# Activation tables of ScalarE: one set with logarithm and exponential kept across stages, other sets asked for at the end of the stage before

## The chip, the cores and the metric

The kernel runs on one core of a Trainium2 chip. The time is device microseconds of one execution, from its start to its end on the device. Each kernel is timed in several runs, and the median is compared; one further execution is recorded by the hardware profiler, and all rows below come from it. The engines of the core are TensorE (PE, matrix products; PEld are its weight loads), VectorE (DVE), ScalarE (ACT, activation functions), GpSimd (POOL) and SyncE (SP, which issues most transfers).

## What is computed

One network of six residual layers over an input of 2 x 128 x 32 x 32, all in float32. Cut to the functions that matter here:

```python
x = L0_conv(x)       # offsets: gelu, tanh; bias: log1p, relu MLP; softmax; then an MLP with gelu
x = L1_conv(x)       # group norm (rsqrt), attention with softmax
t = tokens(x)        # 2 x 1024 tokens of 128
t = t + L2_attn(ln(t))   # 8 heads, softmax with relative positions
t = t + L2_ffn(ln(t))    # trajectory of an ODE (RK4 steps), f(y) = tanh MLP of width 512
t = t + L3_attn(ln(t))   # gated linear attention: log_sigmoid gates, exp of sums
                         #   o = o * rsqrt(mean(o*o) + eps) * g_norm_w * (g * sigmoid(g))
t = t + L3_ffn(ln(t))    # 32 experts, top 2 by sigmoid
ln(v) = (v - mean) / sqrt(var + eps)
```

## The kernel before

Everything stays on chip between the layers. The residual X lies as 128 channels x 2048 columns (2 images x 1024 pixels, NB = 2), and most work goes in NCH = 4 chunks of 512 columns (CH), or in tiles of 128 tokens. PSUM is used as eight banks of 512 columns. The program is written by hand, engine by engine: each layer is one or more stages (class Stage), each with one block in which every engine has its own list of instructions and its own semaphores. Between two blocks all engines meet at a barrier, so a stage begins when the slowest engine of the one before is done. Inside a stage, `wait_ge` and `then_inc` on named semaphores set the order; an engine works through its list in order, and Chain (`link`) waits for an instruction's own result before the next.

The stages in order: l0_bias (prepare and scores), l0_attend, l0_mlp, l1_attention, layer_norm "l2a_norm", l2_attention, l2_guess, l2_sweeps, layer_norm "l3a_norm", l3_gates, l3_chunks, l3_gated_output, layer_norm "l3f_norm", l3_experts.

Places that the change touches:

- l0_prepare, L377: Ln of the distances. l0_attend, L840 to L854: for 16 tiles ScalarE makes Exp and, one tile later, copies the turned probabilities to PT; at the end four copies to ATT feed the projection. l0_mlp, L910 to L916: 16 Gelu.
- l1_attention: the group norm's statistics go VectorE, TensorE, VectorE, TensorE; then VectorE adds eps and takes the reciprocal (L990, L991), ScalarE takes the root (L1045), VectorE makes gain and shift (L994 to L996). Later 16 Exp (L1059).
- layer_norm, three times: TensorE centres four chunks (L1174), ScalarE squares them (L1193), TensorE averages the squares (L1178), ScalarE takes four Ln (L1197) and four Exp with scale -0.5 (L1201), VectorE multiplies (L1185).
- l2_guess: a small norm of two start columns (Sqrt at L1726, reciprocal at L1697), then eight rounds with Tanh (L1730, L1733). TensorE runs products that nobody reads (keep_clock, L1744) while it waits. l2_sweeps: Tanh in a loop (L1938); at its end VectorE writes a flag (L2014) that all engines read to decide on a further sweep; one sweep runs.
- l3_gates: Exp and Ln for the gates (L2119, L2120), later Exp of sums (L2125). l3_chunks: ScalarE only copies outputs (L2229).
- l3_gated_output: TensorE makes four gate products (L2303), ScalarE squares four chunks (L2316) in two buffers, so that number 2 waits for the mean of number 0 (L2306); then four Silu (L2319), four Ln (L2323), four Exp (L2326). VectorE goes chunk by chunk: weighted product (L2332), multiply by the root (L2336); then adds to X (L2339). TensorE projects each chunk (L2309).
- l3_experts: Sigmoid at L2470, then Relu and Copy.

Of the kernel before, what the change touches and what calls it, by code (L numbers as in the profile page):

```python
# [15 lines left out]
ALU = mybir.AluOpType  # L16
# [4 lines left out]
NB = 2  # L21
# [47 lines left out]
class Chain:  # L69
# [5 lines left out]
    def __call__(self, ins):  # L75

        ins.then_inc(self.sem, 1)
        self.n += 1
        self.eng.wait_ge(self.sem, self.n)

# [156 lines left out]
def l0_prepare(st, block, X, PS, W, first, rest, KM, VT, Q, A, WORK, NF, x_in, x_dram):  # L238
# [107 lines left out]
    def _(act):  # L346
# [27 lines left out]
        act.activation(mag[:], flat, ACT.Abs).then_inc(sem("mag"), 1)  # L374
        act.activation(sgn[:], flat, ACT.Sign).then_inc(sem("mag"), 1)
        act.wait_ge(sem("mag"), 2)
        act.activation(mag[:], mag[:], ACT.Ln, bias=1.0).then_inc(sem("logs"), 1)  # L377
# [369 lines left out]
def l0_attend(nc, X, PS, W, SALL, VT, loads):  # L747

    with ExitStack() as ctx:
# [90 lines left out]
        @block.scalar  # L840
        def _(act):
            for s in range(TILES + 1):
                if s < TILES:
                    act.wait_ge(sem("shifted"), s + 1)
                    e = E[:, s % 3].rearrange("p g k -> p (g k)")
                    act.activation(e, e, ACT.Exp).then_inc(sem("exp"), 1)
                if s >= 1:
                    act.wait_ge(sem("back"), s)
                    if s >= 3:
                        act.wait_ge(sem("valued"), s - 2)  # L850
                    act.activation(PT[:, (s - 1) % 2], PS[:, 2 + (s - 1) % 2], ACT.Copy).then_inc(sem("pt"), 1)
            for n in range(NCH):
                act.wait_ge(sem("valued"), 16 if n >= 2 else 8)
                act.activation(ATT[:, n * CH:(n + 1) * CH], PS[:, 4 + n], ACT.Copy).then_inc(sem("att"), 1)  # L854

def l0_mlp(nc, X, PS, W, loads):

    with ExitStack() as ctx:
# [49 lines left out]
        @block.scalar  # L909
        def _(act):  # L910
            for g in range(4 * NCH):
                n, k = divmod(g, 4)
                act.wait_ge(sem("up"), g + 1)
                if n >= 2:
                    act.wait_ge(sem("down"), n - 1)
                act.activation(H[:, n % 2, k], PS[:, g % 6], ACT.Gelu, bias=W["mlp_b1"][:, k:k + 1]  # L916
                               ).then_inc(sem("gelu"), 1)

# [18 lines left out]
def l1_attention(nc, X, PS, W, loads):  # L938

    with ExitStack() as ctx:  # L940
# [32 lines left out]
        def _(dve):  # L973
# [15 lines left out]
            dve.wait_ge(sem("group_var"), 1)  # L989
            link(dve.tensor_scalar(rstd[:], PS[:, 1, 0:NB], 1e-6, None, ALU.add))  # L990
            link(dve.reciprocal(rstd[:], rstd[:]))  # L991
            dve.sem_inc(sem("inverse"), 1)
            dve.wait_ge(sem("root"), 1)
# [49 lines left out]
        def _(act):  # L1043
            act.wait_ge(sem("inverse"), 1)
            act.activation(rstd[:], rstd[:], ACT.Sqrt).then_inc(sem("root"), 1)  # L1045
            for n in range(NCH):
# [107 lines left out]

def layer_norm(nc, name, X, XN, PS, centre, mean, eps, loads=None):

    with ExitStack() as ctx:
# [29 lines left out]
        def _(act):  # L1188
# [9 lines left out]
            for n in range(NCH):  # L1198
                c = slice(n * CH, (n + 1) * CH)
                act.wait_ge(sem("log"), n + 1)  # L1200
                act.activation(R[:, c], R[:, c], ACT.Exp, scale=-0.5).then_inc(sem("inverse"), 1)  # L1201

# [459 lines left out]
def l2_guess(nc, X, O, PS, W, NORM, Y0, Y):  # L1663
    with ExitStack() as ctx:
# [21 lines left out]
        def _(dve):  # L1686
# [9 lines left out]
            dve.wait_ge(sem("root"), 1)  # L1696
            link(dve.reciprocal(R[:], R[:]))  # L1697
            link(dve.tensor_tensor(Y0[:], C[:], R[:], ALU.mult))
# [25 lines left out]
        def _(act):  # L1724
            act.wait_ge(sem("var"), 1)
            act.activation(R[:], PS[:, 4, 0:NB], ACT.Sqrt, bias=NORM["eps"]).then_inc(sem("root"), 1)  # L1726
            for g in range(GUESSES):
# [96 lines left out]
def l2_sweeps(nc, X, X2, PS, W, Y0, Y, loads):  # L1824
# [5 lines left out]
    with ExitStack() as ctx:  # L1830
# [96 lines left out]
        def _(act):  # L1927
            end = act.alloc_register("act_end")
            act.reg_mov(end, STEPS_N)
            with act.Fori(0, end) as sweep:  # L1930
# [12 lines left out]
                reg_wait(act, sem("flag"), sweep + 1, sem("act_passed"))  # L1943
                act.reg_load(end, flag[0:1, 0:1])

        @block.vector
# [228 lines left out]
def l3_chunks(nc, PS, W, KE, KD, V, QM, decay, OT):  # L2175

    with ExitStack() as ctx:
# [45 lines left out]
        @block.scalar  # L2223
        def _(act):
            for t in range(ITILES):
                for b in range(NB):
# [58 lines left out]
def l3_gated_output(nc, X, PS, W, XN, OT, loads):  # L2285

    with ExitStack() as ctx:
# [24 lines left out]
        def _(act):  # L2312
            for n in range(NCH):
                if n >= 2:
                    act.wait_ge(sem("ms"), n - 1)
                act.activation(SQ[:, n % 2], OT[:, col(n)], ACT.Square).then_inc(sem("square"), 1)  # L2316
            for n in range(NCH):
                act.wait_ge(sem("g"), n + 1)
                act.activation(G[:, col(n)], PS[:, n], ACT.Silu).then_inc(sem("silu"), 1)  # L2319

            for n in range(NCH):
                act.wait_ge(sem("ms"), n + 1)
                act.activation(R[:, col(n)], PS[:, 4 + n], ACT.Ln, bias=W["eps"]).then_inc(sem("log"), 1)  # L2323
            for n in range(NCH):
                act.wait_ge(sem("log"), n + 1)
# [3 lines left out]
        def _(dve):  # L2329
            for n in range(NCH):  # L2330
                dve.wait_ge(sem("silu"), n + 1)
                dve.scalar_tensor_tensor(G[:, col(n)], G[:, col(n)], W["g_norm"], OT[:, col(n)], ALU.mult,  # L2332
                                         ALU.mult).then_inc(sem("weighted"), 1)
                dve.wait_ge(sem("root"), n + 1)
                dve.wait_ge(sem("weighted"), n + 1)
# [197 lines left out]
def build(nc, x_dram, packs, offsets, out_dram):  # L2533
    with ExitStack() as ctx:
# [87 lines left out]
        W = pack("l3f", l2f)  # L2622
        layer_norm(nc, "l3f_norm", X, XN, PS, W["centre"], W["mean"], W["eps"])
        l3_experts(nc, X, XN, PS, W, out_dram, stored)
# [20 lines left out]
```

## Time and profile before

| | |
|---|---|
| median of 3 runs | 1673.09 us (1671.84 to 1678.54) |
| the profiled execution | 1676.29 us, its span 1674.4 us |
| PE busy | 1500.5 us, 90% of the span |
| DVE busy | 886.2 us, 53% |
| ACT busy | 872.5 us, 52% |
| POOL busy | 320.8 us, 19% |

The span runs from the first to the last instruction that the profiler recorded; the execution's own time has 1.9 us around it. In the rows below, a time in brackets is how long the engine sat idle before the instruction, with what released it. Without brackets the engine went straight on. Rows of the same line are merged where they follow each other (x4 is four instructions, the second number then the time from the first start to the last end).

### The profile page before, as it was taken

The numbers are of one execution on the slowest core, as the hardware profiler recorded it, in microseconds if no ns is written. First come the engines' busy times: TensorE is split into PE (matmuls) and PEld (weight loads), VectorE is DVE, ScalarE is ACT, GpSimd is POOL, SyncE is SP. The second block draws the span as 40 slices with busy tenths as digits, with TensorE's granted clock in tenths as the row PEclk, the third lists the DMA queues.
The fourth block names the chain that finished last, engine by engine and source line by source line (L and its number), as shares of the span: only waits on it lengthen the run. The fifth ranks groups of instructions, "written<-read, shape, count | busy, mean of one in ns | idle before, by whom it ended". The sixth has DMA issues, their size and how long they took to land. (4 is left out here: it accounts for less than half of the span.)

```text
span 1674.4 us, 29793 instructions
## 1 busy us (share of the span) xinstructions
PE 1500.5 (90%) x12334; PEld 739.5 (44%) x12334; DVE 886.2 (53%) x1364; ACT 872.5 (52%) x1292; POOL 320.8 (19%) x139
## 2 busy tenths in 40 slices
PE   6889999999778997999999999899999999939678
PEld 4322222222243774666666666554444444316333
DVE  2578888888772554677777777110002000258243
ACT  3567777777543435677777776232222222250451
POOL 0746666666220001000000000000000000020000
PEclk9589999999998999799999999899999999979899
DMA  1000000000001003444344431000000000000000
GB/s 65 1 2 2 2 2 2 2 2 2 2 22 77 0 1 118 147 150 162 134 173 177 165 151 39 1 1 0 1 0 0 0 0 0 31 0 4 1 1 25
DMA packets 21089, 69.66 MB, mean 42 GB/s; under 512 B 736, under 2 KB 17248, under 8 KB 18656
## 3 DMA queue, kind: packets, MB, share of 16 engines
q1 hardware_dynamic: 20672, 66.76, 10.7%
q8 instruction: 96, 1.57, 0.4%
q10 hardware_dynamic: 288, 1.05, 0.2%
q14 instruction: 33, 0.27, 0.1%
HBM read 33.21 MB, written 34.60 MB: 40 GB/s over the span
## 5 line engine op out<-in xcount | busy, mean ns | idle before, releaser
L553 POOL TENSOR_TENSOR l_work<-l_a_scores,l_work 128x2048 f32<-128x2048 f32 x64 | 232.9, 3640 | 126.5 <-PE banks L673 126.5
L1909 PE MATMUL banks<-s_h,pack_l2f_l3f 128*128 128x512 f32 x512 | 221.0, 592 | 0.0
L1938 ACT ACTIVATE s_h<-banks,pack_l2f_l3f 128x512 f32<-128x512 f32 x128 | 88.0, 688 | 239.2 <-PE banks L1909 175.7
L1510 ACT ACTIVATE r_e<-banks,r_max 128x512 f32<-128x512 f32 x256 | 162.1, 685 | 51.2 <-DVE r_max L1551 51.1
L613 DVE TENSOR_TENSOR l_work<-banks,sc_negc 128x1024 f32<-128x1024 f32 x128 | 156.2, 1221 | 49.6 <-PE banks L720 33.2
L573 ACT ACTIVATE l_work<-banks,pack_l 128x1024 f32<-128x1024 f32 x128 | 142.7, 1115 | 74.7 <-PE banks L673 73.7
L673 PE MATMUL banks<-l_work,pack_l 32*32 32x512 f32 x4096 | 159.6, 606 | 23.5 <-ACT l_work L573 19.8
L1545 DVE TENSOR_REDUCE r_raw<-banks 128x1 f32<-128x640 f32 (+1 forms) x128 | 109.8, 858 | 90.6 <-PE banks L1435 88.9
L1455 PE MATMUL banks<-pack_l2a,r_e 128*128 128x128 f32 x1024 | 147.5, 285 | 10.4 <-ACT r_e L1510 10.2
L1909 PEld LDWEIGHTS banks<-s_h,pack_l2f_l3f 128*128 128x128 f32 x512 | 97.3, 190 | 122.5 <-issue 122.5
L1435 PE MATMUL banks<-r_k,r_q 32*128 32x128 f32 (+3 forms) x832 | 148.8, 466 | 1.1 <-DVE r_v L1379 1.1
L605 DVE TENSOR_TENSOR l_work<-banks,l_a_scores 128x2048 f32<-128x2048 f32 x64 | 146.0, 2281 | 0.7 <-PE banks L666 0.7
L567 ACT ACTIVATE l_work<-l_work 128x1024 f32<-128x1024 f32 x128 | 134.3, 1052 | 9.6 <-POOL l_work L553 9.6
L1455 PEld LDWEIGHTS banks<-pack_l2a,r_e 128*128 128x128 f32 x1024 | 112.0, 142 | 54.7 <-ACT r_e L1510 46.1
L1964 DVE TENSOR_SCALAR s_k<-banks,pack_l2f_l3f 128x512 f32<-128x512 f32 x12 | 9.0, 750 | 221.8 <-PE banks L1914 221.8
L1435 PEld LDWEIGHTS banks<-r_k,r_q 32*128 32x128 f32 x832 | 87.4, 188 | 71.7 <-issue 55.0
L673 PEld LDWEIGHTS banks<-l_work,pack_l 32*32 32x32 f32 x4096 | 42.1, 103 | 138.2 <-issue 103.3
L2136 POOL MEMSET ga_keep<- 128x1024 f32 x1 | 1.0, 951 | 474.0 <-SPq L2067 474.0
L1559 DVE COPY r_pt<-banks 128x512 f32<-128x512 f32 x128 | 87.9, 687 | 4.1 <-PE banks L1455 3.5
L1518 ACT ACTIVATE r_pt<-banks 128x512 f32<-128x512 f32 x128 | 76.5, 597 | 25.1 <-PE banks L1455 25.1
L1420 PE MATMUL banks<-pack_l2a,r_q 32*128 32x257 f32 x224 | 80.1, 437 | 0.0
L1551 DVE CUSTOM_DVE_ANT_0 banks<-banks,r_band,r_raw 128x384 f32<-128x384 f32 (+1 forms) x128 | 75.9, 593 | 6.3 <-DVE r_raw L1545 0.2
(399 smaller groups left out, 2079.1 us busy)
## 6 DMA issues: line engine op xcount, KB each, us to landing
distances<-r_rd SPq DMA_DIRECT2D x16, 2048.0 KB, 6.5
r_band<-distances SPq DMA_DIRECT2D x16, 1536.0 KB, 7.0
pack_l2f_l3f<-pack_dram_l2f SPq DMA_DIRECT2D x1, 2244.5 KB, 10.4
pack_l2f_l3f<-pack_dram_l3f SPq DMA_DIRECT2D x1, 1248.5 KB, 7.0
residual<-x ACTq DMA_DIRECT2D x2, 512.0 KB, 6.1
out<-residual SPq DMA_DIRECT2D x4, 256.0 KB, 2.0
pack_l<-pack_dram_l SPq DMA_DIRECT2D x1, 945.0 KB, 7.5
pack_l2a<-pack_dram_l2a SPq DMA_DIRECT2D x1, 715.0 KB, 5.5
```

Source lines behind the costliest of these rows:

```text
L553: pool.tensor_tensor(image(H1R[:, (c + 1) % 3]), bc(a, 2, 16), bc(b, 3, HW), ALU.add).then_inc(sem("added"), 1)
L567: act.activation(h, h, ACT.Relu).then_inc(sem("relu"), 1)
L573: act.activation(H2R[:, (2 * c + part) % 3], PS[:, RELU:RELU + 2], ACT.Relu, bias=W["cpb_b2"]).then_inc(sem("h2_relu"), 1)
L605: dve.tensor_tensor(image(H1M[:, c % 2]), bc(b, 3, HW), bc(a, 2, 16), ALU.max).then_inc(sem("h1_max"), 1)
L613: dve.tensor_tensor(image(H2M[:, (2 * c + part) % 3]), image(PS[:, MAX + j:MAX + j + 2]), bc(NEGC[:, j:j + 2, n, i, rows(half)], 3, HW), A ...
L673: ins = pe.matmul(PS[32 * u:32 * u + 32, bank], w2(j), h[32 * j:32 * j + 32, u], start=True, stop=True, tile_position=(32 * j, 32 * u))
L1435: ins = pe.matmul(PS[:, 2 * (t % 2) + a, col:col + n * P], Qm[at, a, h % 2, b * PIX + t * P:b * PIX + (t + 1) * P], K[at, a, b, slot:slot ...
L1455: ins = pe.transpose(PS[:, 4 + h, j * P:(j + 1) * P], E[:, t % 2, c:c + P], W["ident"])
L1510: act.activation(E[:, t % 2, a * CH:(a + 1) * CH], PS[:, 2 * (t % 2) + a], ACT.Exp, bias=mx[:, t % 2:t % 2 + 1], scale=-1.0).then_inc(sem( ...
L1545: dve.tensor_reduce(raw[:, one], v[:, lo:hi], AX.X, ALU.min).then_inc(sem("far"), 1)
L1909: ins = pe.matmul(bank, W["w2"][:, col:col + P], H1[:, c, m], start=(m == 0), stop=(m == HB - 1))
L1938: act.activation(H[:, c, k], PS[:, g % 8], ACT.Tanh, bias=bias).then_inc(sem("tanh"), 1)
```

## The change

- That set is asked for ahead of the Ln in l0_prepare, at the end of l0_mlp, at the end of l2_sweeps and in l3_gated_output between Silu and Ln.
- Gelu's set is asked for in l0_attend after the last Exp (in the last turn of the loop, ahead of the last PT copy), Tanh's in l2_guess after the norm, Silu's at the start of l3_chunks, Sigmoid's at the end of l3f_norm.
- The two roots (group norm, l2_guess) become Ln and Exp with scale -0.5 on ScalarE, each waiting for the one before; VectorE's two reciprocals go.
- In l3_gated_output the squares move from ScalarE to VectorE, Ln and Exp alternate chunk by chunk on ScalarE, and VectorE makes all four weighted products ahead of the four multiplies.

```diff
+LOG_EXP, GELU, TANH, SILU, SIGMOID = ("natural_log_exp_and_others", "gelu_and_others", "exp_and_others",
+                                      "silu_and_others", "sigmoid_and_others")
...
         act.activation(sgn[:], flat, ACT.Sign).then_inc(sem("mag"), 1)
+        act.preload_act_table_set(LOG_EXP)
         act.wait_ge(sem("mag"), 2)
...
                     act.activation(e, e, ACT.Exp).then_inc(sem("exp"), 1)
+                else:
+                    act.preload_act_table_set(GELU)
                 if s >= 1:
                     act.wait_ge(sem("back"), s)
...
                 act.activation(H[:, n % 2, k], PS[:, g % 6], ACT.Gelu, bias=W["mlp_b1"][:, k:k + 1]
                                ).then_inc(sem("gelu"), 1)
+            act.preload_act_table_set(LOG_EXP)
...
-            link(dve.tensor_scalar(rstd[:], PS[:, 1, 0:NB], 1e-6, None, ALU.add))
-            link(dve.reciprocal(rstd[:], rstd[:]))
-            dve.sem_inc(sem("inverse"), 1)
+            dve.tensor_scalar(rstd[:], PS[:, 1, 0:NB], 1e-6, None, ALU.add).then_inc(sem("spread"), 1)
             dve.wait_ge(sem("root"), 1)
...
-            act.wait_ge(sem("inverse"), 1)
-            act.activation(rstd[:], rstd[:], ACT.Sqrt).then_inc(sem("root"), 1)
+            act.wait_ge(sem("spread"), 1)
+            act.activation(rstd[:], rstd[:], ACT.Ln).then_inc(sem("log"), 1)
+            act.wait_ge(sem("log"), 1)
+            act.activation(rstd[:], rstd[:], ACT.Exp, scale=-0.5).then_inc(sem("root"), 1)
...
-def layer_norm(nc, name, X, XN, PS, centre, mean, eps, loads=None):
+def layer_norm(nc, name, X, XN, PS, centre, mean, eps, loads=None, table=None):
...
                 act.activation(R[:, c], R[:, c], ACT.Exp, scale=-0.5).then_inc(sem("inverse"), 1)
+            if table:
+                act.preload_act_table_set(table)
...
             dve.wait_ge(sem("root"), 1)
-            link(dve.reciprocal(R[:], R[:]))
...
-            act.activation(R[:], PS[:, 4, 0:NB], ACT.Sqrt, bias=NORM["eps"]).then_inc(sem("root"), 1)
+            act.activation(R[:], PS[:, 4, 0:NB], ACT.Ln, bias=NORM["eps"]).then_inc(sem("log"), 1)
+            act.wait_ge(sem("log"), 1)
+            act.activation(R[:], R[:], ACT.Exp, scale=-0.5).then_inc(sem("root"), 1)
+            act.preload_act_table_set(TANH)
...
                 act.reg_load(end, flag[0:1, 0:1])
+            act.preload_act_table_set(LOG_EXP)
...
         def _(act):
+            act.preload_act_table_set(SILU)
             for t in range(ITILES):
...
             for n in range(NCH):
-                if n >= 2:
-                    act.wait_ge(sem("ms"), n - 1)
-                act.activation(SQ[:, n % 2], OT[:, col(n)], ACT.Square).then_inc(sem("square"), 1)
-            for n in range(NCH):
                 act.wait_ge(sem("g"), n + 1)
                 act.activation(G[:, col(n)], PS[:, n], ACT.Silu).then_inc(sem("silu"), 1)
-
+            act.preload_act_table_set(LOG_EXP)
             for n in range(NCH):
                 act.wait_ge(sem("ms"), n + 1)
                 act.activation(R[:, col(n)], PS[:, 4 + n], ACT.Ln, bias=W["eps"]).then_inc(sem("log"), 1)
-            for n in range(NCH):
                 act.wait_ge(sem("log"), n + 1)
                 act.activation(R[:, col(n)], R[:, col(n)], ACT.Exp, scale=-0.5).then_inc(sem("root"), 1)
 
         @block.vector
         def _(dve):
+            for n in range(NCH):
+                if n >= 2:
+                    dve.wait_ge(sem("ms"), n - 1)
+                dve.tensor_tensor(SQ[:, n % 2], OT[:, col(n)], OT[:, col(n)], ALU.mult).then_inc(sem("square"), 1)
             for n in range(NCH):
                 dve.wait_ge(sem("silu"), n + 1)
                 dve.scalar_tensor_tensor(G[:, col(n)], G[:, col(n)], W["g_norm"], OT[:, col(n)], ALU.mult,
                                          ALU.mult).then_inc(sem("weighted"), 1)
+            for n in range(NCH):
                 dve.wait_ge(sem("root"), n + 1)
...
-        layer_norm(nc, "l3f_norm", X, XN, PS, W["centre"], W["mean"], W["eps"])
+        layer_norm(nc, "l3f_norm", X, XN, PS, W["centre"], W["mean"], W["eps"], table=SIGMOID)
```

## Rows read from the trace of the kernel before

**Rows 1.** The page's first part: busy time, share of span, count of each engine.

```profile
PE 1500.5 (90%) x12334; PEld 739.5 (44%) x12334; DVE 886.2 (53%) x1364; ACT 872.5 (52%) x1292; POOL 320.8 (19%) x139
```

**Rows 2.** Groups of ScalarE by line: count, busy us, mean ns, idle before.

```profile
L1197 ACT ACT_TABLE_LOAD x3 | 3.8, 1283 | 0.1
...
L1197 ACT ACTIVATE l2a_norm_r<-banks,pack_l2a 128x512 f32<-128x512 f32 x4 | 2.4, 688 | 0.0
...
L1201 ACT ACTIVATE l2a_norm_r<-l2a_norm_r 128x512 f32<-128x512 f32 x4 | 2.2, 618 | 0.0
```

**Rows 3.** Order of time in l2a_norm: start us, us, engine, line, operation.

```profile
632.09 2.89 PE L1178 MATMUL banks<-l2a_norm_sq,pack_l2a 128*128 128x512 f32 x6
...
633.82 1.28 ACT L1197 ACT_TABLE_LOAD   x1
...
635.12 2.42 ACT L1197 ACTIVATE l2a_norm_r<-banks,pack_l2a 128x512 f32<-128x512 f32 x4
...
638.85 2.19 ACT L1201 ACTIVATE l2a_norm_r<-l2a_norm_r 128x512 f32<-128x512 f32 x4
639.51 2.48 DVE L1185 TENSOR_TENSOR normed<-banks,l2a_norm_r 128x512 f32<-128x512 f32 x4 [12.10 <-ACT l2a_norm_r L1201]
```

**Rows 4.** Order of time at the end of l0_attend.

```profile
492.53 0.60 ACT L851 ACTIVATE at_pt<-banks 128x512 f32<-128x512 f32 x1 [0.70 <-PE banks L780]
...
493.18 0.30 PEld L787 LDWEIGHTS banks<-at_pt,l_vt 128*128 128x128 f32 x2 [0.65 <-ACT at_pt L851]
```

**Rows 5.** Order of time at the start of l1_attention.

```profile
528.42 1.28 ACT L1045 ACT_TABLE_LOAD   x1 [7.21 <-PEq L859]
...
534.18 0.20 ACT L1045 ACTIVATE gn_rstd<-gn_rstd 128x2 f32<-128x2 f32 x1 [4.47 <-DVEq L992]
```

**Rows 6.** Order of time in l2_guess, behind the norm.

```profile
1055.36 1.28 ACT L1730 ACT_TABLE_LOAD   x1
...
1058.57 1.33 PE L1775 MATMUL banks<-g_y,pack_l2f_l3f 128*128 128x64 f32 x8
```

**Rows 7.** Order of time at the end of l2_sweeps and the start of l3a_norm.

```profile
1454.39 1.49 PE L1875 MATMUL banks<-pack_l2f_l3f 128*128 128x512 f32 x2
1454.60 0.14 DVE L2014 TENSOR_SCALAR s_flag<-banks 1x1 int32<-1x1 f32 x1
...
1456.15 0.50 PEld L1174 LDWEIGHTS banks<-residual,pack_mlp_l3a 128*128 128x128 f32 x2 [1.46 <-issue]
```

**Rows 8.** Order of time in l3_gates, at the gate's logarithm.

```profile
1486.90 1.28 ACT L2120 ACT_TABLE_LOAD   x1
```

**Rows 9.** Order of time in l3_gated_output.

```profile
1564.88 3.73 PE L2306 MATMUL banks<-go_sq,pack_mlp_l3a 128*128 128x512 f32 x8
...
1567.44 1.28 ACT L2319 ACT_TABLE_LOAD   x1
...
1569.37 0.75 DVE L2332 SCALAR_TENSOR_TENSOR go_g<-go_g,pack_mlp_l3a,gl_o 128x512 f32<-128x512 f32 x1 [14.54 <-ACT go_g L2319]
...
1575.85 2.19 ACT L2326 ACTIVATE go_r<-go_r 128x512 f32<-128x512 f32 x4
...
1580.04 0.75 DVE L2332 SCALAR_TENSOR_TENSOR go_g<-go_g,pack_mlp_l3a,gl_o 128x512 f32<-128x512 f32 x1
...
1580.89 0.69 DVE L2336 TENSOR_TENSOR gl_o<-go_g,go_r 128x512 f32<-128x512 f32 x1
1581.50 2.48 DVE L2339 TENSOR_TENSOR residual<-banks,residual 128x512 f32<-128x512 f32 x4
```

**Rows 10.** Slices: stretch, its us, busy us of each engine, granted clock (PEclk), DMA share.

```profile
638.00:640.00 2.00, 0.00 (x0) 0.00 (x0) 0.48 (x1) 1.99 (x4) 0.00 (x0) 0.81 0.00 0
...
644.00:646.00 2.00, 2.00 (x4) 0.83 (x3) 0.00 (x0) 1.27 (x2) 0.73 (x2) 0.50 0.00 0
646.00:648.00 2.00, 1.84 (x5) 0.53 (x3) 1.53 (x3) 0.98 (x2) 0.00 (x0) 0.98 0.00 0
...
1570.00:1572.00 2.00, 0.00 (x0) 0.00 (x0) 0.12 (x1) 1.98 (x3) 0.00 (x0) 0.77 0.00 0
```

## The prediction

> **What bounds the kernel now.** The program is a row of stages with a barrier between them, so the question for each table load is local: did its stage wait for it? The page's first part says that TensorE is busy 90% of the span and ScalarE 52% [rows 1]; taken alone this would say that ScalarE work is worth nothing. That is an average. I went on in three steps. First the groups of ScalarE: loads stand at 17 lines, 21 loads in all (three each at L1197 and L1201, one each at fifteen others), every one 1283 ns, 26.9 us together [rows 2]. Then the order of time around each, to see what the instruction behind the load waited for. Last the granted clock around the gaps that TensorE has there. The reader should see two kinds of load. One starts as soon as the stage opens or the last work is done, and is over before its data comes. The other stands between two instructions that are both ready, with TensorE and VectorE idle behind it.
>
> **Loads that are covered now.** At L1045 the load runs from 528.42 to 529.70, and the square root behind it starts at 534.18, when VectorE has its variance [rows 5]. L1730 has 1055.36 to 1056.64, while TensorE's first product for Tanh starts only at 1058.57, behind its own clock-keeping products [rows 6]. L359, L846, L916, L1059, L1726, L2125 and L2470 look the same: nine loads of this kind. Taking these away, or asking earlier, gains nothing. The loads of L351 and L377 stay in their places. Ten are left.
>
> **Loads on the path.** A normalisation (three of them, here the first) [rows 3]: Square ends at 633.81 and the load follows at 633.82, Ln runs from 635.12 to 637.54, another load, Exp from 638.85, and VectorE multiplies as the Exps come. Between the end of one ACTIVATE and the start of the next lie 1.31 us. Without a load they overlap: four Ln take 2.42 us and not 4 x 0.688 [rows 2, 3], a pitch of 0.58, so an overlap of 0.11. A load on the path is therefore worth 1.31 + 0.1 = 1.4 us, and two are worth 2.8. Would another wait take over? Ln number 3 needs the last variance product, which ends at 634.98 (632.09 + 2.89); after the change it would start at 633.7 + 3 x 0.58 = 635.4. No. Each normalisation: -2.8.
>
> The Trainium skill, page "ScalarE: Activation LUTs", section "What ACT_TABLE_LOAD costs", gives 1283 ns for the load and a drain of 1380 ns beside it, 2.66 us for every switch. The 1283 ns are the trace's too; the drain isn't, since the ACTIVATE behind stands 1.31 us after the one ahead [rows 3]. By the page's figure the switches on the path would be worth near 1.4 us more each, for ten of them 14 us; the measurement decides.
>
> Gates stage: L2120's load (1486.90) stands between two chained activations, Abs/Exp ahead and Ln behind, and VectorE waits. A chained pair without a load has a gap of 0.03, so it gives back 1.28; the V copies behind Ln waited for nothing, and the load of L2125 is covered by VectorE's scan. All later steps hang on the Ln: -1.3 [rows 8].
>
> **The gated output** is where most is. Before: squares on ScalarE, the last waiting for TensorE, load at 1567.44, Silu, load, Ln, load, Exp to 1578.04 (1575.85 + 2.19), last multiply on VectorE 1580.89 to 1581.58, stage's last add ends 1583.98 [rows 9]. After:
> - Squares go to VectorE: 0.69 for such a product [rows 9] against 0.63, and VectorE sat idle for 14.5 us there [rows 9]. The last one still waits for TensorE and ends near 1567.5. Behind that wait stand the four weighted products.
> - Silu no longer waits for squares, only for its own product. The last of these ends as the next product of TensorE begins, 1564.88 [rows 9], plus 0.2: Silu over by 1565.7. The Silu table is asked for in the chunk stage, whose ScalarE has an idle start.
> - The table request: 1565.7 to 1567.0. Only Ln number 0 waits for it; its mean is two passes of 0.43 after 1564.88, 1565.9 with the way to ScalarE.
> - Ln and Exp alternate, each Exp waiting for its Ln: 0.69 + 0.03 + 0.62 - 0.10 = 1.24 per chunk. Exp number 3 ends at 1567.0 + 4 x 1.24 + 0.1 = 1572.05.
> - VectorE: weighted products 1567.5 + 4 x 0.66 + 0.1 = 1570.2 (0.75 each [rows 9], 0.09 overlap); multiplies from there at 0.60, the last waits for Exp number 3: 1572.1 to 1572.8.
> - From the last multiply to the end the stage took 2.40 (four adds, 2.48 from first to last [rows 9]); kept, this gives 1575.2 against 1583.98. -8.7. TensorE needs 4 x 0.86 from 1571.0 at the high clock, 1574.4, just in time. At the low one 1577.8 and the gain is -5.3: the upper bound.
>
> **What the early requests cost.** The load is asked for at the end of a stage, where something may be last already.
> - l0_attend (Gelu): between the second last and the last copy of PT. Before, the last copy waits 0.70 for TensorE and starts at 492.53, and the product behind waits for that copy [rows 4]. The load runs 491.83 to 493.11: copy, last product, projection and adds come 0.6 later. At L916 the load was covered, so nothing is given back: +0.6.
> - l0_mlp: ScalarE sits idle 7.2 us until the next stage opens at 528.42 [rows 5]: 0.
> - Group norm: Ln (0.20) + 0.03 + Exp (0.20) take the place of reciprocal (0.17), a step over and the root (0.20): between -0.1 and +0.3, I take 0 since the two chains are both 0.5 long.
> - l2_guess: +0.03 on VectorE, hidden with the Tanh load behind TensorE until 1058.57 [rows 6]; without that cover 0.03 and 0.
> - End of the sweeps: nothing in the trace shows when ScalarE leaves its loop. The flag is written at 1454.74; the barrier falls 0.27 after TensorE's last product (1454.39 + 1.49 = 1455.88) [rows 7]. ScalarE comes between those two times; with the load it arrives at 1456.1 to 1457.1, that is +0.2 to +1.3. I take the middle, +0.7.
> - l3f_norm (Sigmoid): ScalarE's Exps end 0.95 before VectorE's last multiply (641.04 and 641.99 in the row of the first norm [rows 3]); a load of 1.28 there makes ScalarE last by +0.3. L2470 was covered: nothing back. If the barrier doesn't wait for a load, this term and the one before are 0.
>
> Sum: 3 x (-2.8) - 1.3 - 8.7 + 0.6 + 0.7 + 0.3 = **-16.8 us**. The profiled execution took 1676.29 (span 1674.4), 3.2 above the median of 1673.09; it goes to 1659.5, and the median to **1656.3**.
>
> **The clock.** TensorE's gap of 7.3 us at a norm lets its granted clock fall: it is 0.81 in the mean from 638 to 640, 0.50 (the 1.2 GHz level) in the slices from 640 to 646, and 0.98 behind, with TensorE back at work from 642.3 [rows 10]. So some 3.7 us of work run at half speed, costing 1.8. The change cuts these gaps to 4.5, and that of the gated stage from 8.7 to 2.3. The fall came about 4 us after TensorE stopped at 634.98, at the gated stage some 2.5 us after its last mean (0.77 from 1570 to 1572) [rows 10]; so I count neither gain nor loss in the sum, and put it in a rival.
>
> **Rivals.**
> A. The clock stays at 2.4 GHz through all four gaps: 4 x 1.8 = 7 us more, 1649.3. For it: the gaps are shortened by 38 to 74%. Against: gaps of 4.5 us are still longer than the time the fall took. Chance 0.10.
> B. TensorE becomes the bound of the gated output at the low clock (-5.3 in place of -8.7) and the requests cost their upper bounds (+0.6 more): -12.8, 1660.3. For it: the clock fell 2.5 us after the last product there. Chance 0.13.
> C. Slower: the loads go on being placed by function, and the explicit requests come on top. Before, Ln is given a table without Exp although one with both exists: every Ln and Exp pair of the norms has two loads [rows 2, 3]. Then the alternation in the gated stage takes 0.69 + 1.3 + 0.62 + 1.3 = 3.93 per chunk: from 1568.3 to 1582.7, +4.7 against 1578.04; group norm +1.3, requests +1.6: +7.6, 1680.7. It decides at the second load in front of an Exp. Against: Tanh, Exp, Relu and Copy that a loaded set serves have no load of their own, so a set is kept while it serves. Chance 0.03.
> The Trainium skill's page "ScalarE activation tables: per-element evaluation and per-set limits", section "Table sets in the compiler and the runtime", says that loads are placed for the greedy longest run. By that rule Ln and Exp of a norm would share one load already and the change would gain one and not two per norm. The trace has two [rows 2].
> D. The sweeps stop when the last change is small enough; one sweep now, 336 us. Roots made as exponentials shift the start value a little; if the test failed, a second sweep would give some 1993. It acts on guess and sweep alike, so chance 0.01.
>
> **How the numbers follow.** Forecast 0.73. Its own spread: the runs of before span 6.7 us, and the parts uncertain by a microsecond or two, so about 1652 to 1661. The range reaches to A's and B's sides: **1648 to 1664**. Half a per cent (8.4 us) is what a measurement here can tell from no change. Faster by more (under 1664.7): forecast, A and most of B, 0.92. Within: 0.06. Slower: half of C, and D, 0.02.
>
> **What would show it.** Ten loads and not 21, none at L1197 or L1201's places; norms from Square to first Exp 2.8 shorter; last multiply of the gated stage some 9 us after the last square mean and not 14; a Gelu load ahead of the last PT copy; l3_experts opening behind a ScalarE load. The forecast fails if Ln and Exp are still loaded apart, if TensorE runs low through the gated projection, or if the barrier gaps grow where loads were added.

## The result, and the profile after

| | before | after |
|---|---|---|
| median | 1674.68 us (11 runs, 1671.84 to 1678.54) | 1667.14 us (11 runs, 1663.41 to 1671.83) |
| profiled execution | 1676.29 us, span 1674.4 | 1664.98 us, span 1663.1 |
| PE busy | 1500.5 us | 1504.4 us |
| ACT busy | 872.5 us | 856.3 us |

The ratio is 0.9955, with a 95% interval of 0.9939 to 0.997: faster by 7.5 us where 16.8 were forecast. (Ratios leave disturbed runs out, so they need not equal the quotient of two medians.) The two profiled executions differ by 11.3 us.

The loads did what they should. ScalarE's groups of after by line (count, busy us, mean ns, idle before) have ten loads; these are the requests that stand at the end of a stage, in l0_attend, l2_sweeps and the norm, and the one inside the gated stage:

```profile
L853 ACT ACT_TABLE_LOAD x1 | 1.3, 1283 | 0.0
...
L1957 ACT ACT_TABLE_LOAD x1 | 1.3, 1283 | 3.2 <-DVE s_flag L2027 3.2
...
L2330 ACT ACT_TABLE_LOAD x1 | 1.3, 1283 | 0.0
L1211 ACT ACT_TABLE_LOAD x1 | 1.3, 1283 | 0.0
```

The first norm of after, in order of time (start, us), against [rows 3]: Ln starts while the last Square ends, Exp while the last Ln ends.

```profile
632.36 0.60 ACT L1201 ACTIVATE l2a_norm_sq<-banks 128x512 f32<-128x512 f32 x1 [1.12 <-PE banks L1186]
632.85 2.41 ACT L1205 ACTIVATE l2a_norm_r<-banks,pack_l2a 128x512 f32<-128x512 f32 x4
635.13 2.21 ACT L1209 ACTIVATE l2a_norm_r<-l2a_norm_r 128x512 f32<-128x512 f32 x4
635.82 2.48 DVE L1193 TENSOR_TENSOR normed<-banks,l2a_norm_r 128x512 f32<-128x512 f32 x4 [9.24 <-ACT l2a_norm_r L1209]
```

The gated stage of after, against [rows 9]: the load of the common set at 1565.64, Ln and Exp in turn from 1566.93, VectorE's multiplies from 1570.00, its last add over at 1575.17:

```profile
1561.32 3.67 PE L2317 MATMUL banks<-normed,pack_mlp_l3a 128*128 128x512 f32 x8 [0.63 <-PEq L2190]
...
1565.64 1.28 ACT L2330 ACT_TABLE_LOAD   x1
...
1566.93 0.69 ACT L2333 ACTIVATE go_r<-banks,pack_mlp_l3a 128x512 f32<-128x512 f32 x1
1567.35 2.73 DVE L2345 SCALAR_TENSOR_TENSOR go_g<-go_g,pack_mlp_l3a,gl_o 128x512 f32<-128x512 f32 x4
1567.65 0.63 ACT L2335 ACTIVATE go_r<-go_r 128x512 f32<-128x512 f32 x1
...
1570.00 2.72 DVE L2350 TENSOR_TENSOR gl_o<-go_g,go_r 128x512 f32<-128x512 f32 x4
...
1570.74 3.70 PE L2323 MATMUL banks<-gl_o,pack_mlp_l3a 128*128 128x512 f32 x8 [2.13 <-DVE gl_o L2350]
...
1572.64 2.53 DVE L2353 TENSOR_TENSOR residual<-banks,residual 128x512 f32<-128x512 f32 x4
```

Where, then, did the rest go? With a barrier between stages the two traces can be laid side by side, stage by stage. The table gives each stage's length, from the moment when the last engine reached the end of one block to the same moment of the next, and behind it how long TensorE had the low clock in it (granted 0.50, 1.2 GHz). All in us:

| stage | before | low | after | low | difference |
|---|---|---|---|---|---|
| l0_bias | 443.62 | 51.2 | 442.68 | 58.0 | -0.94 |
| l0_attend | 53.85 | 6.8 | 54.38 | 6.8 | +0.54 |
| l0_mlp | 29.62 | 0 | 29.62 | 0 | 0 |
| l1_attention | 99.28 | 10.2 | 98.83 | 6.8 | -0.45 |
| l2a_norm | 14.41 | 1.9 | 11.55 | 0 | -2.86 |
| l2_attention | 410.24 | 25.5 | 408.31 | 20.5 | -1.9 |
| l2_guess | 63.42 | 6.8 | 71.07 | 23.9 | **+7.65** |
| l2_sweeps | 340.96 | 0.7 | 340.96 | 0.4 | 0 |
| l3a_norm | 14.96 | 4.7 | 14.40 | 7.6 | -0.56 |
| l3_gates | 26.27 | 9.2 | 25.43 | 11.8 | -0.85 |
| l3_chunks | 62.16 | 12.7 | 63.19 | 14.4 | +1.03 |
| l3_gated_output | 23.92 | 13.7 | 13.75 | 0 | -10.2 |
| l3f_norm | 14.63 | 2.7 | 11.49 | 0 | -3.1 |
| l3_experts | 75.25 | 4.2 | 75.59 | 3.4 | +0.34 |

The differences sum to the 11.3 us. Without l2_guess they are 19.0. In l2_guess the instructions are nearly the same; the clock isn't. The whole stage in one slice (length, busy us of PE, PEld, DVE, ACT, POOL, then the granted clock), first before, then after:

```profile
1051.32:1114.74 63.42, 58.01 (x417) 38.71 (x418) 13.09 (x35) 16.69 (x53) 0.00 (x0) 0.95 0.00 1
```

```profile
1045.70:1116.77 71.07, 65.67 (x417) 43.05 (x418) 12.92 (x34) 16.14 (x53) 0.00 (x0) 0.83 0.00 1
```

The same stage of after in order of time. Its clock-keeping products (L1756) run from 1049.01 to 1052.68, and the sixteen products of L1797 take 3.68 us in each of the first two rounds:

```profile
1049.01 3.67 PE L1756 MATMUL banks<-pack_l2f_l3f 128*64 128x256 f32 x8
...
1052.61 1.97 PE L1787 MATMUL banks<-g_y,pack_l2f_l3f 128*128 128x64 f32 x8
...
1055.56 3.68 PE L1797 MATMUL banks<-pack_l2f_l3f,g_h 128*64 128x256 f32 x16
...
1067.22 3.68 PE L1797 MATMUL banks<-pack_l2f_l3f,g_h 128*64 128x256 f32 x16
```

In before the clock-keeping products (L1744) took the same 3.67 us, but the sixteen products of the first round (L1785) took 1.95:

```profile
1054.97 3.67 PE L1744 MATMUL banks<-pack_l2f_l3f 128*64 128x256 f32 x8
...
1060.41 1.95 PE L1785 MATMUL banks<-pack_l2f_l3f,g_h 128*64 128x256 f32 x16
```

Shorter slices of after (the same columns) show the clock at 0.50 from 1047.8 to 1071.6 and 1.00 behind:

```profile
1047.80:1051.10 3.30, 2.85 (x9) 1.85 (x9) 0.87 (x5) 1.75 (x3) 0.00 (x0) 0.50 0.00 0
...
1058.00:1071.60 13.60, 12.63 (x58) 7.92 (x56) 1.21 (x3) 2.29 (x7) 0.00 (x0) 0.50 0.00 1
1071.70:1080.00 8.30, 7.82 (x65) 5.56 (x64) 1.56 (x4) 1.92 (x7) 0.00 (x0) 1.00 0.00 0
```

In before the stage had the low clock only up to 1059:

```profile
1052.30:1059.00 6.70, 5.73 (x16) 3.58 (x17) 1.41 (x8) 2.35 (x3) 0.00 (x0) 0.50 0.00 0
1059.10:1068.00 8.90, 8.42 (x71) 5.78 (x72) 1.21 (x3) 2.63 (x10) 0.00 (x0) 1.00 0.01 2
```

So the question for the chip was why the clock stayed low here: by chance in each execution (theory 1), because of the stage's new norm (theory 2), or because of where the stage now falls in time against the moments at which the clock changes (theory 3).

### The profile page after: what moved, and what is told of

It reads as the page before. It is cut to its first block and busy times, and to the rows that moved or that the text cites. A ratio compares the mean times of both kernels' runs of the same rounds, so it can differ in the third digit from the quotient of the medians.

```text
span 1663.1 us, 29783 instructions
## 1 busy us (share of the span) xinstructions
PE 1504.4 (90%) x12334; PEld 743.0 (45%) x12334; DVE 888.5 (53%) x1366; ACT 856.3 (51%) x1279; POOL 320.7 (19%) x139
## 5 line engine op out<-in xcount | busy, mean ns | idle before, releaser
L1520 ACT ACTIVATE r_e<-banks,r_max 128x512 f32<-128x512 f32 x256 | 161.9, 684 | 51.2 <-DVE r_max L1561 51.2
L1465 PE MATMUL banks<-pack_l2a,r_e 128*128 128x128 f32 x1024 | 147.8, 286 | 10.3 <-ACT r_e L1520 10.2
## 6 DMA issues: line engine op xcount, KB each, us to landing
pack_l2f_l3f<-pack_dram_l2f SPq DMA_DIRECT2D x1, 2244.5 KB, 10.2
```

Source lines behind the costliest of these rows:

```text
L1465: ins = pe.transpose(PS[:, 4 + h, j * P:(j + 1) * P], E[:, t % 2, c:c + P], W["ident"])
L1520: act.activation(E[:, t % 2, a * CH:(a + 1) * CH], PS[:, 2 * (t % 2) + a], ACT.Exp, bias=mx[:, t % 2:t % 2 + 1], scale=-1.0).then_inc(sem( ...
```

## The experiments

### Twice the same kernels

> The changed kernel once more, for a second profiled execution and more times. Theory 1 (drawn clock): in the first profile l2_guess ran 23.9 us at the low clock and was 7.65 us longer than before, with the same instructions; where the clock falls there is drawn anew in each execution, so this profile should show another amount, and the stages whose low time differs should differ by about half of that low time or less. Theory 2 (caused by the change): the new norm in l2_guess or the Tanh load sets it, so this profile shows l2_guess again near 71 us with 20 us or more at the low clock. Either way the median ratio to the kernel before stays near 0.9955.

> The kernel before once more, for a second profile. Theory 1: l2_guess (63.4 us, 6.8 at the low clock in the first profile) takes another amount of low clock, up to the 24 us of the changed kernel, and up to 71 us. Theory 2: it stays at 62 to 64 us with under 10 us low. The stages that the change didn't touch differ between the two profiles of before by their low clock alone.

after_again: median 1663.41, ratio 0.9929 (0.9905 to 0.9953), 11.9 us less than before where the first timing had 7.5; the two intervals of this one kernel overlap in part. Its l2_guess took 71.07 us with 23.9 low, to the hundredth as in the first profile. before_again: 63.39 with 6.8. Theory 1 fails for the profiled executions: they repeat stage for stage. From l2a_norm to l3a_norm no stage differs by more than 0.03 us between the two profiles of either kernel, but for l2_attention of the changed one (408.31 and 408.60). Ahead of l2a_norm they do differ: l0_bias of the changed kernel took 442.68 and 444.91, l0_attend 54.38 and 53.41, as its 6.8 us of low clock came 7.4 and 3.7 us behind the stage's start. Theory 2 isn't touched by this.

### One part alone, and all but one

order_back, the changed kernel with the gated stage in the old order:

```diff
+                if n >= 2:
+                    act.wait_ge(sem("ms"), n - 1)
+                act.activation(SQ[:, n % 2], OT[:, col(n)], ACT.Square).then_inc(sem("square"), 1)
...
                 act.activation(R[:, col(n)], PS[:, 4 + n], ACT.Ln, bias=W["eps"]).then_inc(sem("log"), 1)
+            for n in range(NCH):
                 act.wait_ge(sem("log"), n + 1)
```

> The changed kernel with the gated stage in its old order: squares on ScalarE, all Ln ahead of all Exp, VectorE chunk by chunk; the table requests stay. By the sums: norms 3 x -2.8, gates -1.3, in the gated stage two of three loads go from the path (-2.8), requests +0.6 +1.1 +0.3: -10.5 us, ratio 0.9937, against 0.989 for the whole change by the same sums. If the gated stage's new order really gave its 6 us in time (and not only in one profile), this kernel is 6 us slower than the changed one. If those 6 us are given back later by the clock, it is equal to it within 2 us.

gated_only, the kernel before with the gated stage's part of the change, and nothing else:

```diff
+            act.preload_act_table_set(SILU)          # l3_chunks
...
+            act.preload_act_table_set(LOG_EXP)       # l3_gated_output, with the new order of both engines
```

> The kernel before with only the gated stage changed (squares on VectorE, Ln and Exp alternating under one set, Silu asked for in the chunk stage); that set then also serves the last norm. By the sums: gated stage -8.7, last norm -2.8: -11.5 us, ratio 0.9931. If the gain is lost to the clock in l2_guess, which lies ahead of everything changed here, this kernel should lose nothing there and gain as much as or more than the whole change (7.5 us). If the gain is lost at the end, in l3f_norm and l3_experts, it gains under 5.

order_back: 0.9972 (0.9957 to 0.9987), 4.7 us less than before in the ratio where 10.5 were expected. Against the changed kernel in the same timing (0.9929, after_again) it is 7.2 us slower, where 6 were expected if the new order's gain is real in time. gated_only: 0.9939 (0.9922 to 0.9956), 10.2 us where 11.5 were expected, more than the whole change reached in its first timing (in the second, 0.9929, the intervals overlap). The profiles say why: order_back has l2_guess at 71.07 us with 23.9 low, gated_only at 63.37 with 6.8. The gated part is worth what was forecast (15.45 and 11.49 us for its two stages, against 23.92 and 14.63). What is lost is lost in l2_guess, ahead of the gated part, and in these four kernels only where the table loads of the stages up to it are changed.

### Is it the stage's own norm?

guess_root_back, the changed kernel with the old root in l2_guess:

```diff
-            act.activation(R[:], PS[:, 4, 0:NB], ACT.Ln, bias=NORM["eps"]).then_inc(sem("log"), 1)
-            act.wait_ge(sem("log"), 1)
-            act.activation(R[:], R[:], ACT.Exp, scale=-0.5).then_inc(sem("root"), 1)
+            act.activation(R[:], PS[:, 4, 0:NB], ACT.Sqrt, bias=NORM["eps"]).then_inc(sem("root"), 1)
...
+            link(dve.reciprocal(R[:], R[:]))
```

> The changed kernel with the square root and the reciprocal back in l2_guess's norm; the table of Sqrt is then loaded at the start of the stage, covered, all else as changed. Theory 2 (the new norm pushes the stage to the low clock): l2_guess 63 to 64 us, 6.8 low. Theory 3: 71 us and 23.9 low as with the exponential, since the stage starts at the same time.

```profile
1042.56:1113.63 71.07, 65.66 (x417) 43.07 (x418) 13.07 (x35) 17.20 (x53) 0.00 (x0) 0.83 0.00 1
```

71.07 us, clock 0.83: the same with the old root. Theory 2 is out. (Ratio 0.9937, 0.9912 to 0.9962.)

### Moving the stage in time

guess_later adds useless work to the changed kernel, ahead of VectorE's first step of the stage:

```diff
+            for _ in range(4):
+                link(dve.memset(AO[:], 0.0))
             dve.wait_ge(sem("heads"), 1)
```

> The changed kernel with 1.9 us of useless work (four memsets of a tile that is overwritten later) ahead of VectorE's first step in l2_guess. Theory 3 (where the stage falls against the clock's decision): in all three kernels with the shorter norms l2_guess ran 71.07 us with 23.9 at the low clock, in all three with the long norms 63.4 with 6.8; the clock returned early only where nearly all of the 3.67 us of keep_clock products lay between two changes of the clock. With 1.9 us more they should lie so again: l2_guess 65 to 67 us, 14 us low or less, and the whole 2 to 6 us faster than the changed kernel although work was added. Theory 2 (the new norm of l2_guess) or a plain sum of work: 1.9 us slower, l2_guess 73 us.

Its slice of l2_guess, and the products in question:

```profile
1047.32:1112.45 65.13, 57.53 (x417) 38.47 (x418) 14.85 (x38) 15.58 (x52) 0.00 (x0) 0.95 0.00 1
```

```profile
1053.15 3.43 PE L1758 MATMUL banks<-pack_l2f_l3f 128*64 128x256 f32 x8
1056.51 1.10 PE L1789 MATMUL banks<-g_y,pack_l2f_l3f 128*128 128x64 f32 x8
...
1058.12 1.95 PE L1799 MATMUL banks<-pack_l2f_l3f,g_h 128*64 128x256 f32 x16
```

The four memsets delayed the chain by 2.2 us (TensorE's wait for the first step of VectorE grew from 0.25 to 2.44), and the stage became 5.9 us shorter: the first round finds the high clock (L1799 takes 1.95 again). Ratio 0.9905 (0.9883 to 0.9927), clear of the changed kernel's first timing; from its second, 0.9929, it is 4 us away with overlapping intervals.

The slices of the clock say more exactly than the expectation what differs. The clock-keeping products lie inside one stretch of low clock in either kernel (before: low from 1052.25 to 1059.08; after: from 1047.76 to 1071.65), so that doesn't tell them apart. In the four profiles with some 63.4 us in l2_guess (before, before_again, gated_only, requests_later) the clock fell 0.6 to 0.9 us behind the stage's start and the products began 2.7 to 3.2 us behind the fall. In the six with 71.07 it fell 2.0 to 2.1 us behind the start, and the products began 1.2 to 1.4 behind the fall. In guess_later it fell 2.06 behind the start as well, but the products came 3.8 behind the fall, and the low clock lasted 6.8 us.

The same four memsets in the kernel before:

> The kernel before with the same 1.9 us of useless work ahead of VectorE's first step in l2_guess that made the changed kernel faster. Theory 3 (where the stage falls against the clock's decisions): in before the keep_clock products lie well (63.4 us, 6.8 low); 1.9 us later they lie as in the changed kernel, so l2_guess takes 63.4 + 1.9 + 5 to 8 = 70 to 73 us with over 15 us low, and the kernel is 7 to 10 us slower than before. If only the work counts: 65.3 us with 6.8 low, 1.9 us slower.

```profile
1049.00:1115.03 66.03, 58.66 (x417) 39.19 (x418) 15.02 (x39) 16.85 (x53) 0.00 (x0) 0.92 0.00 1
```

In the profile this did not come as theory 3 expected: the stage is 66.03 us with 10.2 low, 2.6 longer and not 7 to 10, near the plain sum of work. The median of twelve runs is 1685.17 against 1677.09, 8.1 us more; the ratio, 1.0036 (1.0012 to 1.006), gives 6.0. The twelve fall into two groups. Seven took 1683.98 to 1689.05 us with a mean granted clock of 0.946 to 0.949; five, the profiled one among them, took 1669.6 to 1678.73 with 0.952 to 0.958. So the long ones are the ones with more low clock, and the profile shows a short one. That their low clock lies in l2_guess, as theory 3 has it, isn't shown.

guess_keep8 leaves the stage where it is and doubles the clock-keeping products (`for _ in range(8): keep_clock()`). By theory 3 the stage was to have 6.8 to 10.2 us low and 67 us at most, and the whole was to be some 4 us faster than the changed kernel:

> The changed kernel with eight instead of four keep_clock calls ahead of the first round of l2_guess, 7.3 us of products instead of 3.67. [...] If the low clock has another cause: 3.7 us slower, 75 us.

```profile
1051.23 6.36 PE L1756 MATMUL banks<-pack_l2f_l3f 128*64 128x256 f32 x16
```

l2_guess 65.58 us with 6.8 low, ratio 0.991 (0.9889 to 0.9932). The clock fell 2.0 us behind the start as in the changed kernel and came back while the added products ran; they took 6.36 us in place of 3.67, 2.7 more, and the stage is 5.5 shorter. In time it is 3 us from after_again (0.9929), with overlapping intervals.

### The requests

requests_later puts three of the early requests back behind the barrier:

```diff
-                else:
-                    act.preload_act_table_set(GELU)
...
         def _(act):
+            act.preload_act_table_set(GELU)
             for g in range(4 * NCH):
...
         def _(act):
+            if table:
+                act.preload_act_table_set(table)     # LOG_EXP for l3a_norm; Sigmoid is loaded where it is used
             for n in range(NCH):
                 act.wait_ge(sem("centred"), n + 1)
```

> The changed kernel with three table requests moved from the end of a stage to the start of the next: Gelu into l0_mlp, the log and exp set into l3a_norm, Sigmoid to the place where it is needed. By the first profile: l0_attend 0.6 shorter, the barrier ahead of l3a_norm no longer waits for a load that ended 1.1 us after the others, l3f_norm 0.3 shorter: -2.0 us. Against: Gelu's request moves the later stages against the clock, so l1_attention and l2_guess may take another low time. If l2_guess stays at 71 us, -2; if the shift of 0.6 us releases it, -9.

Ratio 0.9897 (0.9873 to 0.9922), the gain that was forecast for the change itself. l0_attend is back at 53.85, l3a_norm at 12.11, and l2_guess at 63.36 with 6.8 low. The shorter l0_attend by itself isn't what released it: in after_again l0_attend took 53.41 and l2_guess 71.07. What differs next to l2_guess is l2_attention, 409.81 with 23.9 low here against 408.31 and 408.60 with 20.5 in the two profiles of the changed kernel; behind it the clock fell 0.8 us after the start of l2_guess and not 2.0. Which of the steps ahead sets this isn't isolated. But now the gated stage takes 17.09, not 13.75, and its projection ran at the low clock, 5.34 us for what took 3.70:

```profile
1563.46 5.34 PE L2321 MATMUL banks<-gl_o,pack_mlp_l3a 128*128 128x512 f32 x8 [2.12 <-DVE gl_o L2348]
...
1568.84 0.69 DVE L2351 TENSOR_TENSOR residual<-banks,residual 128x512 f32<-128x512 f32 x1 [0.17 <-PE banks L2321]
```

That is the first half of rival B of the prediction, in another kernel than it was written for.

### Filling the gaps

warm_gaps is requests_later with useless products in TensorE's gaps; before_warm_gaps has them in the kernel before (six at the gated place).

```diff
+            pe.wait_ge(sem("log"), 1)                # layer_norm
+            for _ in range(4):
+                pe.matmul(PS[:, 4], centre, X[:, 0:CH], start=True, stop=True)
...
+            for _ in range(18):                      # l3_gates
+                pe.matmul(PS[:, 6], W["wv"], XN[:, 0:CH], start=True, stop=True)
...
+            pe.wait_ge(sem("silu"), NCH)             # l3_gated_output
+            for _ in range(2):
+                pe.matmul(PS[:, 3], W["wg"], XN[:, col(3)], start=True, stop=True)
```

> The kernel with the later requests (requests_later) and useless products for TensorE in its gaps: four behind the last variance product of each norm, two ahead of the gated projection, eighteen behind the V products of l3_gates, all in banks already read. Theory 3: the clock doesn't fall in these gaps, so the stages behind give back what they lost at the low clock: l2_attn some 3 to 5 us, l3_gates 1 to 2, l3_chunks 1 to 3, l3_gated 17.1 back to 13.8: 8 to 13 us less than requests_later, if l2_guess isn't moved to a bad place by it. If the useless products hold up a barrier or a needed product, the stage they stand in shows it.

> The kernel before with useless products in the same gaps (six ahead of the gated projection). Does the low clock behind the gaps cost the kernel before as much as the changed one? If the loss is a matter of the gaps, it gains 4 to 9 us in l2_attn, l3_gates, l3_chunks and l3_gated. If the loss is particular to the changed kernel, nothing. l2_guess starts some 1 to 3 us earlier against the clock and may fall to 71 us, which would take the gain away.

warm_gaps: 0.9871 (0.985 to 0.9892), 4.4 us under requests_later with overlapping intervals. In the profiles, against requests_later the gated stage is back at 13.76 (17.09), l3_chunks 59.85 (63.48), l3_experts 73.87 (76.64), l2_attention 408.58 (409.81), l3_gates 24.00 (24.68); and l2_guess is again

```profile
1045.92:1116.99 71.07, 65.66 (x417) 43.03 (x418) 12.92 (x34) 16.15 (x53) 0.00 (x0) 0.83 0.00 1
```

12 us won, 7.7 given back there. before_warm_gaps: 0.9983 (0.997 to 0.9996), 3 us less. Of the 4 to 9 us expected in its four stages the profile shows 3.5 (l2_attention 408.51 and the gated stage 22.01, nearly nothing in the other two), and its l2_guess fell to 71.07 too; that profiled execution, 1681.39 us, was the slowest of the twelve. So 71.07 us is no property of the changed kernel: the kernel before has it too when what lies ahead of the stage is shifted, here with the old tables throughout and with norms as long as before (l2a_norm 14.40).

warm_keep8 adds the eight keep_clock calls to it:

> warm_gaps with eight instead of four keep_clock calls in l2_guess. In warm_gaps the gaps were filled, but l2_guess fell back to 71.07 us with 23.9 low; with eight calls on the changed kernel it was 65.6 with 6.8. Theory 3: l2_guess 65.6 again, all other stages as in warm_gaps, so 5.5 us less than it: a ratio to the kernel before near 0.984. If the fill of the gaps and the longer products don't add up: l2_guess stays at 71 plus 3.7.

l2_guess is 65.14 with 6.8 low, near the 65.6 expected, but not by the way expected: here the clock fell 0.8 us behind the stage's start, as in the kernels that take 63.4 us with four calls, so the eight calls were not needed. l2_attention had changed too (409.83 with 23.9 low, 408.58 with 20.5 in warm_gaps). The ratio is 0.985 (0.9822 to 0.9879), the lowest measured and 25 us under before, but its interval overlaps that of warm_gaps, and the median fell by 0.8 us and not by 5.5. In the profiles l0_bias (446.57 against 442.66), l3_chunks (+1.7), l3_experts (+1.7) and l2_attention (+1.3) took it back. That the longer products are worth their place on top of the filled gaps isn't shown.

## Why the prediction was wrong, by its own steps

- **Which loads are on the path**: right. Ten loads, none in a norm. The norms with both loads gone: 14.41 to 11.55 in the first (-2.86, forecast -2.8); 14.96 to 14.40 in l3a_norm, which also has the late barrier and 2.9 us more low clock (12.11 in requests_later, -2.85); and 14.63 to 11.49 in the last one, which had 2.7 us of low clock before and none after, with 0.32 coming back at the barrier behind Sigmoid's load: from VectorE's end to TensorE's first product of l3_experts it was 1.22 us before and is 1.54 (-2.8 and +0.3 forecast). The drain of 1380 ns that the Trainium skill gives ("ScalarE: Activation LUTs", section "What ACT_TABLE_LOAD costs") doesn't show here either: in the gated stage the load starts at 1565.64 and Ln at 1566.93, 1.29 us later.
- **The gated stage**: -8.7 forecast, -10.2 in the profile. The steps came as written (load at 1565.64, forecast 1565.7; first Ln 1566.93, forecast 1567.0; multiplies from 1570.00, forecast 1570.2; projection 1570.74, forecast 1571.0). The rest is the start: the stage's gate products took 3.67 us at the high clock, where before they took 5.37. gated_only, with 3.4 us low, has 15.45: -8.5. So the steps were right and the closeness of the total is in part luck, since it hangs on the clock there: requests_later, with the same steps, has 17.09, -6.8.
- **The early requests**: in l0_attend the last copy of PT starts 1.91 us after the one before it, in both profiles of after, and 1.30 before: +0.61 (forecast +0.6). The stage as a whole moves more than that with its low stretch: +0.54 in one profile and -0.44 in the other. End of the sweeps: the load begins at 1457.51, 0.75 after the flag, and holds up the barrier; the next stage opened 1.32 us after the last other engine was ready, before 0.44. That is +0.9, inside +0.2 to +1.3, where 0.7 was taken.

```profile
1456.62 0.14 DVE L2027 TENSOR_SCALAR s_flag<-banks 1x1 int32<-1x1 f32 x1
...
1457.51 1.28 ACT L1957 ACT_TABLE_LOAD   x1 [3.18 <-DVE s_flag L2027]
...
1459.09 2.90 PE L1182 MATMUL banks<-residual,pack_mlp_l3a 128*128 128x512 f32 x3 [1.50 <-PEq L1842]
```

- **Gates**: -1.3 forecast, -0.85 seen with 2.6 us more low clock; -1.6 in requests_later with 2.4 us less than before.
- **The clock**: the step that failed. The prediction looked at four gaps that the change cuts, found a price of 1.8 us each, and counted 0 for the sum. It left out that an edit shifts every later stage against the clock, also those that it doesn't touch, and that of all stages l2_guess answered most. One round of it took 6.6 us at the high clock and 11.7 at the low one, and once low it stayed so for 23.9 us where before it came out of it after 6.8. That the clock could move the result was said (rivals A and B), for the gaps that are cut; the shift, its place and its size were not: +7.65 in one stage, against a forecast of nothing there. The other stages together gave 19.0, 2.2 more than the forecast. The text's sentence on l2_guess, "hidden with the Tanh load behind TensorE until 1058.57", was right on the load and said nothing of the clock-keeping products that it pointed to.
- **Rivals C and D** fell: one set served both functions and one sweep ran.
- **The range** (1648 to 1664) was too narrow on the slow side: apart from C and D, the only slower case priced the gated projection and the requests. The profiled execution (1664.98) lies 1 us outside, the median 3. The text also took half a per cent (8.4 us) for the least that can be told from no change and gave 0.06 to a result within it; the result, 7.5 us, is one, and its interval of 0.15% to either side tells it from none.

What stays open: between the profiles the gain is 11.3 us, between the medians 7.5 in the first timing and by the ratio 11.9 in the second, and executions of one kernel spread over 7 to 13 us (after_again 1655.39 to 1668.71) while its profiled ones repeat to the hundredth of a us in l2_guess. That a shift of the stage, or more products in it, ends the long low stretch is shown by profiles (guess_later, guess_keep8), and by the times against the first timing of the changed kernel alone. It isn't shown which of the changed loads moved l2_guess against the clock, nor which stages make the spread.

## What to carry to other kernels

A table load is worth its 1.3 us plus an overlap of 0.1 only where both neighbours are ready; the order of time around each load tells that. Asking early at the end of a stage can make the load the last thing the barrier waits for, so the start of the next stage is the better place when ScalarE waits there anyway. On a kernel whose TensorE work is thin in places, forecast the clock by stages, and for every stage behind the edit, not only for the gaps that it changes. Before judging an edit of a few us, compare the stages of both traces one by one with their low time: in a stage whose code is unchanged or nearly so, a move of 7 us beside 17 us more low time points to the clock, and a few products that keep it up may be worth more than the edit.

## What the runs showed of the hardware

- The same work can stay at the low clock over three times as long: l2_guess took 71.07 us (23.9 low) or 63.4 (6.8 low) with nearly the same instructions. What differs in the profiles is how far behind the fall of the clock the 3.67 us of clock-keeping products began, 1.2 to 1.4 us in the first case and 2.7 to 3.2 in the second. Six profiles of five kernels had the first, four profiles of three kernels the second, and guess_later, guess_keep8, warm_keep8 and before_guess_later came out at 65.1 to 66.0 with added work.
- Adding 1.9 us of useless work made l2_guess of the changed kernel 5.9 us shorter (ratio 0.9905, against 0.9955 and 0.9929), and the same work made the kernel before slower by 8.1 us in the median (6.0 by the ratio), with the lower granted clock in the seven long executions.
- The barrier waits for a table load in flight: the stage behind the sweeps opened as the load ended, 1458.79, plus 0.3.
- From l2a_norm on, the profiled executions of a kernel repeat their low stretches at the same places, counted from the stages, though the first fall of the clock came at 17 to 19 us in some profiles and at 37 to 42 us in others, of one kernel too.
